# Evicting the transposed activations on ScalarE instead of VectorE, and issuing the weight casts one at a time behind the small constants

## What is computed

```python
xn = layernorm(x)
# recurrent part
xr = rmsnorm(xn) * norm_w
f  = maximum(sigmoid(xr @ w_forget.T), 0.9);  i = 1 - f
v  = xr @ w_input.T;                          o = sigmoid(xr @ w_output.T)
h_t = f_t[..., None] * h_{t-1} + i_t[..., None] * v_t[..., None, :]
s   = xn + o * h.sum(-1)
# feed-forward part: one of 4 experts per token, chosen by argmax
e   = argmax(xn @ W_router)
h   = gelu(xn @ W1[e] + b1[e])
y   = layer_norm(h @ Wo + bo + xn)
out = x + s * silu(y)
```

## Time and profile before

| | us |
|---|---|
| median of 2 runs, slowest core | 3365.69 (3362.53 to 3368.86) |
| the profiled execution's own time | 3382.36 |
| its span on the slowest core (core 4) | 3380.5 |
| spans of the 8 cores | 3344.9 to 3380.5 |
| part A on core 4: start to the first matmul behind the barrier | 798.0 |
| TensorE busy | 2893.4 (86%) |
| VectorE busy | 705.9 (21%) |
| ScalarE busy | 474.8 (14%) |

### The profile page before, as it was taken

One profiled execution on the slowest core, in us unless ns is written; L12 is line 12 of the kernel. 1 busy time (PEld: TensorE's weight loads), 2 busy tenths in 40 slices (PEclk: granted clock), 3 DMA queues, 4 the chain that ended last, 5 costly groups with the idle time before them and its releaser, 6 DMA issues.

```text
span 3380.5 us, 31954 instructions; the slowest of 8 cores (3344.9 to 3380.5 us)
## 1 busy us (share of the span) xinstructions
PE 2893.4 (86%) x12904; PEld 1251.7 (37%) x13160; DVE 705.9 (21%) x1273; ACT 474.8 (14%) x741; POOL 244.8 (7%) x349
## 2 busy tenths in 40 slices
PE   0137777785999999999999999999999999999994
PEld 0013333332444444444434444444444444444442
DVE  0126655654001200210031012101200210021003
ACT  1112232211001110111002011101110111002001
POOL 1024352400000000000000000000000000000000
PEclk9977888897999999999999999999999999999997
DMA  9999999923444453345434543444353345524531
GB/s 131 126 104 114 130 119 126 131 55 138 149 139 147 149 184 134 132 161 170 166 125 143 181 146 141 149 175 146 141 187 137 132 154 175 186 100 137 185 127 63
DMA packets 262384, 476.12 MB, mean 141 GB/s; under 512 B 204700, under 2 KB 204700, under 8 KB 216988
## 3 DMA queue, kind: packets, MB, share of 16 engines
q1 hardware_dynamic: 54080, 335.58, 29.1%
q0 software_dynamic: 182816, 132.18, 23.9%
q10 hardware_dynamic: 25344, 6.29, 2.1%
HBM read 482.44 MB, written 81.79 MB: 167 GB/s over the span
## 4 chain that ended last, share of the span: by engine, by line
PE 68%; DMA 5%; DVE 1%; issue 1%; ACT 1%; DVEq 0%; SPq 0%; ACTq 0%; POOL 0%; POOLq 0%
PE pre L630 52%; PE y2b L651 7%; PE y2a L651 7%; DMA w1sl<-w1s 4%; PE pre L637 2%; DVE y L687 0%; DMA wosl<-wos 0%; DVE y L683 0%; PE y2b L656 0%; PE pmu L664 0%; PE psq L587 0%; DVEq L96 0%; PE y2a L656 0%; PE pmu L580 0%; ACT g_bf L769 0%
## 5 line engine op out<-in xcount | busy, mean ns | idle before, releaser
L630 PE MATMUL pre<-maskedA,w1sl 128*128 128x512 bf16 x8022 | 1819.7, 382 | 53.7 <-DMA w1sl<-w1s 43.8
L630 PEld LDWEIGHTS pre<-maskedA,w1sl 128*128 128x128 bf16 x8192 | 786.1, 98 | 1022.9 <-issue 127.2
L793 ACT ACTIVATE interA<-pre 128x512 bf16<-128x512 f32 x256 | 152.9, 597 | 1753.9 <-PE pre L637 1753.7
L651 PE MATMUL y2a<-interA,wosl 128*128 128x512 bf16 x1007 | 238.2, 394 | 2.0 <-ACTq L96 1.1
L651 PE MATMUL y2b<-interA,wosl 128*128 128x512 bf16 x1007 | 224.4, 379 | 1.9 <-DMA wosl<-wos 1.1
L457 PE MATMUL pj<-xn_fm,wiT 128*128 128x512 bf16 x496 | 154.9, 465 | 77.5 <-DMA wiT<-wnat_s 42.4
L162 POOL DMA_DIRECT2D w1s<-w x256 | 187.4, 763 | 298.3 <-issue 298.3
L726 DVE COPY mask_bf<-pmb 4x512 bf16<-4x512 bf16 x8 | 3.3, 412 | 977.9 <-PE pmb L597 977.9
L457 PE MATMUL pj<-xn_fm,wfT 128*128 128x512 bf16 x504 | 123.3, 403 | 71.4 <-ACT f_fm L240 49.9
L651 PEld LDWEIGHTS y2a<-interA,wosl 128*128 128x128 bf16 x1024 | 102.8, 101 | 134.3 <-issue 22.7
L560 POOL DMA_DIRECT2D wosl<-wos x64 | 33.8, 529 | 1575.3 <-PE y2a L651 1293.9
(11 more groups left out here) (121 smaller groups left out, 1231.8 us busy)
## 6 DMA issues: line engine op xcount, KB each, us to landing
w1sl<-w1s SPq DMA_DIRECT2D x256, 1024.0 KB, 4.9
wosl<-wos POOLq DMA_DIRECT2D x64, 1024.0 KB, 5.8
w1s<-w POOLq DMA_DIRECT2D x256, 128.0 KB, 16.3
x_a<-x SPq DMA_DIRECT2D x8, 2048.0 KB, 15.4
x_b<-x SPq DMA_DIRECT2D x8, 2048.0 KB, 15.2
out<-y POOLq DMA_DIRECT2D x8, 2048.0 KB, 8.1
wos<-wo POOLq DMA_DIRECT2D x8, 1024.0 KB, 51.1
xnbf_s<-xn_fm SPq DMA_DIRECT2D x8, 1024.0 KB, 22.7
```

What stands on the lines that cost most here:

```text
L630: ins = te.matmul(pre[b][:, :], w1sl[gi % 2][:, off:off + 128], maskedA[:, (e * KC + k) * TT:(e * KC + k + 1) * TT], start=first, stop=False)
L651: ins = te.matmul(y2[b][:, :], wosl[wi_ % 2][:, ic * 128:(ic + 1) * 128], interA[:, ic * TT:(ic + 1) * TT], start=(ic == 0), stop=False)
L793: ti(sc.activation(interA[:, i_abs * TT:(i_abs + 1) * TT], pre[b][:, :], AF.Gelu), "pre_F%d" % b, 1)
```

## The change

Three edits, all in part A.

1. GpSimd issues `wr` and `b1` first, and then the three weight casts, each one only when the cast before it has landed (`s_wn0`, `s_wn1`). The DMAs for `Wo` and `W1` follow as before.
2. The 8 copies of the transposed activations move from VectorE to ScalarE, at the head of its tile loop, ahead of the square root of the next tile and, in tile 0, ahead of the 24 transposing DMAs. With them move the signals `trA_F0`, `trA_F1` and the drain with `ss_xnev`.
3. VectorE's multiplication by the rms factor waits for each group's `trA_F` instead of standing behind all eight copies.

```diff
-                    for widx, src in enumerate([wiw, wf, wow]):
-                        ti(g.dma_start(out=wnat_s[widx * D:(widx + 1) * D, :], in_=src[:, :]),
-                           "s_wn%d" % widx, 16)
                     wr_src = wr[:, :].rearrange("(k p) e -> p k e", p=128)
                     ti(g.dma_start(out=wr_bf[:, :].rearrange("p (k e) -> p k e", k=KC),
                                    in_=wr_src), "s_wr", 16)
                     ti(g.dma_start(out=b1t_bf[:, :], in_=b1[:, :]), "gp_cst", 16)
+                    for widx, src in enumerate([wiw, wf, wow]):
+                        if widx > 0:
+                            W(g, "s_wn%d" % (widx - 1), 16)
+                        ti(g.dma_start(out=wnat_s[widx * D:(widx + 1) * D, :], in_=src[:, :]),
+                           "s_wn%d" % widx, 16)
...
                     for t in range(NT):
+                        W(sc, "s_xnw%d" % (t % 2), 16 * (t // 2))
+                        W(sc, "sv_s", t - 1)
+                        W(sc, "sv_x2ev", t - 1)
+                        W(sc, "s_lgR", t - 1)
+                        for k in range(KC):
+                            g_ = 8 * t + k
+                            p_ = g_ % 2
+                            W(sc, "trA_R%d" % p_, g_ // 2 + 1)
+                            ti(sc.copy(xn_fm[t % 2][:, k * TT:(k + 1) * TT],
+                                       trA[p_][:, :]), "trA_F%d" % p_, 1)
+                        DR(sc, "ss_xnev")
                         if t + 1 < NT:
                             sqrtf(t + 1)
...
                     for t in range(NT):
-                        W(v, "s_xnw%d" % (t % 2), 16 * (t // 2))
-                        W(v, "sv_s", t - 1)
+                        W(v, "trB_R1", t + 1)
                         for k in range(KC):
                             g_ = 8 * t + k
                             p_ = g_ % 2
-                            W(v, "trA_R%d" % p_, g_ // 2 + 1)
-                            ti(v.tensor_copy(xn_fm[t % 2][:, k * TT:(k + 1) * TT],
-                                             trA[p_][:, :]), "trA_F%d" % p_, 1)
-                        DR(v, "ss_xnev")
-                        W(v, "trB_R1", t + 1)
-                        for k in range(KC):
+                            W(v, "trA_F%d" % p_, g_ // 2 + 1)
                             ti(v.scalar_tensor_tensor(xn2_fm[:, k * TT:(k + 1) * TT],
```

## The result

The changed kernel took 3316.9 us, the median of 11 runs, and the kernel before 3372.9, the median of 10; the ratio is 0.982, with a 95% interval of 0.980 to 0.984. So the change saves 1.8%, 56 us between the medians and 60 by the ratio, and the prediction had 53 us and 3313 us. Some runs, in which one die was disturbed, are in these medians but not in the ratios, and of one profile further down only the undisturbed cores are read. The profiled execution took 3308.3 us.

The account below looks back on a forecast made before the run. Part A's first 798 us were at stake: VectorE's chain at tile starts, `x` and the vectors queued behind casts. 33 us (tiles) plus 20 (start) made 53, from 3365.7 to 3313 us; range 3290 to 3342.

Parts of the forecast that it names:

- Tiles 1 to 7: Term for edits 2 and 3: 4.9 us at each of six tile starts, 3.5 at tile 7, 33 us in sum.
- The step with VectorE's chain: At a tile's start, multiplications follow the statistics beside ScalarE's 591 ns copies, find every group ready, end 4.9 us earlier.
- TensorE still waits 4 us for the eviction of `v`: Sign at a tile's start: TensorE's 4 us wait stays, since it hangs on VectorE's tail, which moves as a block.
- more than both: Rival, chance 0.14: transposes begin 30 us earlier and shorter gaps spare TensorE's slow clock, 3 us in four tiles; 3291 us.
- the lower bound of the term: Tiles 1 to 7: nothing is gained if a tile's pace is set elsewhere, by a late `x`.
- The start: Term for edit 1, before tile 1: transposing DMAs issued at 93 instead of 118, less 5 us, so 20 us gained.
- the other reading: At the start: the last vector lands at 46, in the first gap between casts, and the transposes gain 28 us.
- 5 off for the load of `x(2)`: Deduction at the start: transposes now meet the load of `x` for tile 2, so 25 us earlier leaves 20.
- room under the cap: End of part A: last feed-forward casts at about 710, barrier at 745, so room for some 35 us more.
- the start gives nothing: Rival, chance 0.17: vectors miss the gaps and land near 98, or the transposes set the pace; 3337 us.
- the copy's engine decides: Rival, chance 0.07: ScalarE's longer copies pace transposes and multiplications, each tile loses 1.3 us, 11 in all; 3357 us.
- the vectors starve: Rival, chance 0.04: at the start the four vectors stand behind all three casts, the last landing at 134; 3373 us.

Follow-up runs that it names:

- the second pair: The kernel before and the changed kernel, both unedited, measured once more on another chip; ratios 1.0013 and 0.9797 to the kernel before.
- edits 2 and 3 alone: The changed kernel with the weight casts put back where they were, without their waits; ratio 0.9874 to the kernel before.
- the earlier loads: The changed kernel with each load of `x` issued as soon as its buffer is free, a tile earlier; ratio 0.981 to the kernel before.
- the version with 43.56 us of wait: The changed kernel with GpSimd waiting for all 24 transposing DMAs before the casts of `Wo` and `W1`; ratio 0.9713 to the kernel before.
- edit 1 alone: The kernel before with only the reordered weight casts and the waits between them; ratio 0.9926 to the kernel before.

## Why the prediction was right, step by step

**The total** was right: 53 us forecast, 56 measured between the medians and 60 by the ratio, inside the range, at 3317 us for 3313. But that it came so close is luck. The two terms that were added up met a gain in part A of 67 us on the mean core, in both pairs of profiles, and the second pair's ratio (0.9797) is worth 68 us; the first measurement gave less on the slowest core, for a reason that these runs don't show. The terms:

- *Tiles 1 to 7, 33 us forecast, 33.8 measured.* The step with VectorE's chain was right: multiplications right behind the statistics, at ScalarE's copies of 587 ns (591 by the earlier trace rows), no waits for a copy; 5.15 us where I had 4.9 (5.0 on the mean of tile 6), and tile 7 gave 4.1 (77.3 to 73.2) where I had 3.5. Edit 3's share I had right without saying that it was nearly all of it: awaiting all eight copies, edit 2 gives 5 us in the whole loop.

```profile
L242 ACT COPY xn_fm<-trA x64: 587/587/593, 63.1 to 656.3; 128x512 bf16<-128x512 bf16 x64
```

- *"TensorE still waits 4 us for the eviction of `v`"* failed. The wait in the tile shown is 1.88 us, and 17.2 in seven tiles in the place of 27.8. I had moved the tail as a block, which is right for VectorE: its multiplications end 7.9 us before the restart in both traces (441.80 to 449.70 and 458.18 to 466.08). But TensorE doesn't move with it. Counted from the broadcast, it ended its sixteen matmuls at 18.1 us before (445.70, which is 449.70 less the wait) and at 15.1 now (464.20), 3 us earlier, while the restart came 5.15 earlier; the 2.1 between are the shorter wait. The prediction's own numbers had it: it put the first projection at 436.3, 1.7 us earlier, and the restart 4.9 earlier, and so the wait could not stay at 4. By itself the shorter wait changes no end.
- *TensorE's clock, priced at nothing in the forecast, about 1.5 us a tile measured.* In tile 6 the 48 matmuls behind the restart and the projection with `woT` took 1.5 us less at a mean granted clock of 0.88 for 0.84. In the tile shown, the 48 matmuls take 10.52 us at 1.00 where the same ones before stood in this row, at 0.50:

```profile
449.70 13.40 PE L457 MATMUL pj<-xn_fm,wiT 128*128 128x512 bf16 x47 [4.00 <-DVE v_bf L334]
```

  That is the extreme of the spread, and the mean over all tiles is 11.9 for 12.5. I had the clock as a rival ("more than both"), by way of shorter gaps, and argued against it with the sentence that failed. But the wait's length doesn't decide the clock: behind 3.23 us it was 1.00, behind 2.04 it was 0.66, in the same kernel. Why the mean clock rose is open.
- *What gave it back.* A tile that waits for nothing else gained 6.6 us, and six of them with the 4.1 of tile 7 make 43.7, what edits 2 and 3 alone show (43); 33.8 came in the profile after. Six such tiles and the seventh are 6 x 71.4 + 77.3 = 505.7 us before, so the loop's 520.4 held 14.7 of other waits; after, 6 x 64.8 + 73.2 = 462.0, and 486.6 held 24.6. Those 10 us more are waits for the load of `x`, which is late next: with the earlier loads the loop took 462.4, the sum without any wait. I had named a late `x` as the lower bound of the term, and gave it no price. Two errors of about 10 us, the clock and `x`, cancelled.
- *The start, 20 us forecast, 33 measured.* The steps were of the right kind, and mis-sized. `x` complete at 21.5 (`x_a` at 12.8), the cast of 19.4 us, the gap of 5: all near. But I had the last vector land in the second gap, at 69; it landed in the first, at 44.9, which I had named as the other reading. I had the pace in the gap about right (2638 packets in 6 us, 440 a microsecond, for 485), but the gap had at least the 6 us of that row in the place of 5, and some 1360 had passed before it, 366 of them in the row above and 636 in the last microsecond ahead of the gap, and so only a few were left when the second cast came. From there the transposes were issued at 68.6, found the third cast until 88, and gained the 28 that I had worked out for just this case: TensorE's first projection came 27.9 us earlier. I then took 5 off for the load of `x(2)`; no run here shows such a loss, and the 27.9 leave no room for it. The choice of the gap, 3 us, and this deduction, 5, are the larger part of the 13 us. The other 5 were gained inside tile 0, from the first projection to tile 1 (93.7 us in the place of 98.7), for which I had no term; that is less than two profiles of one kernel differ by.
- *Part B unchanged, and room under the cap.* Right. The last feed-forward casts of q0 ended at 670 to 691 where I had 710, 29 to 40 us ahead of the barrier, near the 35 us of room that I had, and the barrier's wait, 12.53 us, is the old one. That there was some room and not more is shown by the version with 43.56 us of wait.

**The rivals.** That the start gives nothing is refuted by edit 1 alone, with tile 1 at 219.7. That the copy's engine decides is refuted by edits 2 and 3 alone (0.9874). The rule of the Trainium skill, "ScalarE: Activation LUTs", Rules for kernel authors, has the direction right for the copy, 587 against 425 ns, and no say here, since the work left the late engine for an idle one. That the vectors starve is refuted by their landing at 44.9, but its mechanism is real: without the waits between the casts they do starve, and land at 101.5. "More than both" was right that the transposes begin 30 us earlier and that the clock gains (1.5 us in each of six tiles, 9 in all, where it had 12), wrong in tying the clock to the wait, and its time of 3291 missed by 26 us, since it too had no price for the late `x`.

**What stays open.** Why TensorE's mean clock rose, as said. The first profile of the changed kernel has a tile loop of 487 us, the second one 478, edits 2 and 3 alone 477. How much of that is edit 1's, with more of q0's traffic beside the tiles, and how much differs from one chip or execution to another, these runs don't tell. Nor do they tell whether the earlier loads of `x` are worth anything in the whole time.

## What to carry to other kernels

Before a transfer is moved earlier, find out who really waits for it: here nothing read the vectors when VectorE stood waiting for them, and moving that one wait brought tile 1 forward by most of what reordering the casts did. Small transfers hardly moved beside a large one in another queue, but they passed in the gap behind it, so a wait between two large casts can be a cheap priority. Work taken from a late engine paid here only when that engine's next step no longer waited for all of it, and after each such step one looks for what is late next, here first the load of `x`, then the casts ahead of the barrier. And a striking pair of rows is not yet the mean: the clock at one restart went from 0.50 to 1.00, that of the whole tile from 0.84 to 0.88.

## What the runs showed of the hardware that was not expected

- DMA transposes moved 171 packets a microsecond beside the casting DMAs of q0 and 627 alone; the casts 214 and 377. Taking turns packet by packet would leave each 235 (an estimate from the rates alone), so both lose somewhat more than their turn.
- A queue of 4-byte packets moved 15 in 4 us beside a cast that moved 15 of its own, and 2638 in the 6 us after it. A queue that has its DMA issued can be as good as not started: 37 packets of the transposes in the first 16 us.
- TensorE's granted clock in the same place of the program was not set by the length of the stall ahead of it: 0.50 behind 4.00 us and 1.00 behind 1.88, but also 1.00 behind 3.23 and 0.66 behind 2.04. At 1.00 the 48 matmuls took 10.52 us, behind the stall of 2.04 us 12.21, and behind that of 4.00 us 13.40.
